# Attention scores contracted over 32 rows in four row groups, with odd score units copied by ScalarE and subtracted by GpSimd

## The reference, cut to what matters

```
for layer in (0, 1):
    h = layernorm(x); Q, K, V = h Wq, ctx Wk, ctx Wv      # 16 heads of width 8
    scores = Q K^T / sqrt(8)    (+ bias[64, 64] and a key padding mask, layer 1 only)
    x = x + tanh(g) * (softmax(scores) V) Wo
    x = x + tanh(g') * ffn(layernorm(x))
```

## Time and profile before

| | us |
|---|---|
| median of 3 executions (190.67 to 191.41) | 191.34 |
| the profiled execution's own time | 190.85 |
| its span in the profile | 189.0 |
| PE busy in the span | 171.1 |
| DVE busy | 146.5 |
| ACT busy | 79.8 |
| POOL busy | 78.5 |

### The profile page before, as it was taken

How to read it: one execution, slowest core, us unless ns; L and a number is a source line. 1 busy time by engine, 2 the same in 40 slices (tenths; PEclk the granted TensorE clock), 3 DMA queues, 4 the chain that set the end, 5 groups by cost and what they waited for, 6 DMA issues and landing times.

```text
span 189.0 us, 4325 instructions
## 1 busy us (share of the span) xinstructions
PE 171.1 (91%) x1606; PEld 95.1 (50%) x1606; DVE 146.5 (77%) x364; ACT 79.8 (42%) x178; POOL 78.5 (42%) x88
## 2 busy tenths in 40 slices
PE   7579869999998979889998969989999998998994
PEld 2134326555577436356665933333555555643593
DVE  0589999889989799285666396799989996769942
ACT  3262355665563252255554001335644556245300
POOL 8429994004043764006666603154674454110000
PEclk9966999999999999999999997999999999999999
DMA  6999999930002010454421030000000000000012
GB/s 163 336 419 350 263 259 235 184 124 2 3 0 24 29 57 30 81 123 77 79 51 31 6 111 3 0 2 2 3 0 3 0 3 0 3 0 0 3 39 72
DMA packets 19558, 15.01 MB, mean 79 GB/s; under 512 B 3493, under 2 KB 18087, under 8 KB 19282
## 3 DMA queue, kind: packets, MB, share of 16 engines
q1 hardware_dynamic: 18370, 13.17, 28.2%
q0 software_dynamic: 736, 1.07, 1.8%
q10 hardware_dynamic: 432, 0.50, 1.1%
HBM read 7.82 MB, written 6.85 MB: 78 GB/s over the span
## 4 chain that ended last, share of the span: by engine, by line
PE 56%; DVE 22%; issue 7%; DMA 5%; POOL 5%; ACT 3%; SPq 0%; POOLq 0%; DVEq 0%
PE bank L878 47%; PE bank L955 6%; DMA xr<-x_in 3%; POOL rstd L311 2%; DVE oT L641 2%; DVE Sa L634 2%; POOL Sx L385 2%; PE bank L1194 2%; DVE Vx L607 2%; DVE mx L636 2%; DVE st L567 1%; DMA big<-sorted_rows 1%; DVE mx L624 1%; DMA sorted_rows<-Pe,slot 1%; ACT xnT L421 1%
## 5 line engine op out<-in xcount | busy, mean ns | idle before, releaser
L878 PE MATMUL bank<-Kx,QT 128*64 128x512 f32 x128 | 35.8, 644 | 2.5 <-DVE Sx L627 2.2
L311 POOL TENSOR_TENSOR rstd<-ve,nhalf 128x2 f32<-128x2 f32 x16 | 11.7, 730 | 54.5 <-DVE ve L573 54.4
L462 ACT ACTIVATE Pe<-Sx 128x512 f32<-128x512 f32 x32 | 20.1, 630 | 24.7 <-POOL Sx L385 15.1
L955 PEld LDWEIGHTS bank<-cst,Pe 128*128 128x128 f32 x128 | 13.5, 140 | 24.3 <-ACT Pe L462 13.0
L373 POOL DMA_INDIRECT routed_rows<-big x15 | 14.8, 984 | 19.7 <-DVE big L843 12.7
L466 ACT ACTIVATE big<-bank 128x512 f32<-128x512 f32 x32 | 18.8, 587 | 8.8 <-PE bank L955 8.7
L955 PE MATMUL bank<-cst,Pe 128*128 128x128 f32 x128 | 20.9, 286 | 0.7 <-ACT Pe L462 0.6
L385 POOL TENSOR_TENSOR Sx<-Sa,mx 128x512 f32<-128x512 f32 x16 | 16.8, 1051 | 11.3 <-DVE mx L636 11.3
L641 DVE RECIPROCAL oT<-bank 128x128 f32<-128x128 f32 x16 | 15.2, 952 | 3.5 <-PE bank L878 3.4
L415 ACT ACTIVATE xn<-xr,nmr,rstd 128x128 f32<-128x128 f32 x20 | 9.2, 486 | 19.4 <-DVE nmr L579 19.3
L878 PE MATMUL bank<-zb 128*32 128x512 bf16 x47 | 14.9, 458 | 2.5 <-DVE bo L598 1.4
(11 more groups left out here) (111 smaller groups left out, 305.2 us busy)
## 6 DMA issues: line engine op xcount, KB each, us to landing
sorted_rows<-empty SPq DMA_DIRECT2D x1, 4686.0 KB, 29.5
wgu<-rgu SPq DMA_DIRECT2D x1, 2048.0 KB, 10.3
wdn<-rdn SPq DMA_DIRECT2D x1, 1024.0 KB, 12.3
big<-sorted_rows SPq DMA_DIRECT2D x15, 66.0 KB, 2.2
ctxT<-ctx_in SPq DMA_DIRECT2D x2, 256.0 KB, 4.6
xr<-x_in SPq DMA_DIRECT2D x2, 256.0 KB, 5.2
wf<-ffn SPq DMA_DIRECT2D x1, 512.0 KB, 5.2
Kx<-KT SPq DMA_DIRECT2D x16, 32.0 KB
```

Of the source, the lines that this page charges most:

```text
L311: pool.tensor_tensor(rstd[:, w], ve[:, w], nhalf[:, w], ALU.pow).then_inc(s_pow, 1)
L462: act.activation(Pe[:, u % 3, :], Sx[:, u % 2, :], ACT.Exp).then_inc(s_exp, 1)
L878: return pe.matmul(o, l, r, start=first, stop=last, **k)
L955: ins = pe.transpose(bank[2 + u % 2][:, m * P:(m + 1) * P], Pe[:, u % 3, m * P:(m + 1) * P], ident)
```

## The change

* K is spread into 4 copies (`HG`) in place of 8: copy j keeps in each group of 32 rows the rows of that group's head j. Q lies once, unpadded. `scores` contracts over 32 rows: a unit is now 4 matmuls (2 row groups by 2 batches) of 256 columns in place of 2 of 512. A unit's 512 columns straddle two PSUM banks, one for each row group (`pair`, `heads`). Even units use row groups 0 and 1 and banks 0 and 1, odd units row groups 2 and 3 and banks 2 and 3. Transposes move to banks 4 and 5; values have one bank (6), output projections bank 7.
* Even units go on as before in both layers (`unit_e`). Odd units are copied out of PSUM by ACT (`score_evac`); in layer 1 POOL adds bias and mask to the copy (`add_bias`); DVE takes the maximum of it (`max_o`); POOL subtracts in both layers (`subtract`).
* PE's order is new: both scores of pair n, odd transposes of pair n-1, values of pair n-1, even transposes of pair n, output projection of pair n-2.
* Both projections of V stand before the first scores; V is cleared at the outset, and the memset of QT is gone. Q's pieces 2 and 3 are projected together. Sorted rows `xs` have a buffer of their own, so the token DMA no longer waits. Banks and waits of later stages are renumbered to match.

```diff
+        pair = [ctx.enter_context(nc.psum_tensor(f"pair{i}", [P, 1024], F32)) for i in range(2)]
+        heads = [pair[i][:, 256:768].rearrange("p (h k) -> p h k", h=HH) for i in range(2)]
...
-            pool.memset(QT[:, :, :], 0.0).then_inc(s_zq, 1)
...
-            pool.memset(Vx[:, 0:HH, :, :], 0.0).then_inc(s_zv, 1)
+            for c in range(CH):
+                pool.memset(Vx[:, c * HH:(c + 1) * HH, :, :], 0.0).then_inc(s_zv, 1)
...
+            def add_bias(n):
+                pool.wait_ge(s_ev, PAIRS + n + 1)
+                sa = Sa[:, n % 2, :].rearrange("p (h k) -> p h k", h=HH)
+                pool.tensor_tensor(sa, sa, mid_bcast(bm[:, n, :], HH), ALU.add).then_inc(s_addo, 1)
+
+            def subtract(layer, n, hh):
+                N = PAIRS * layer + n
+                pool.wait_ge((s_mxe, s_mxo)[hh], (n, N)[hh] + 1)
+                if N:
+                    pool.wait_ge(s_exp, 2 * N - 1 + hh)
+                pool.tensor_tensor(Sx[:, hh, :].rearrange("p (h k) -> p h k", h=HH),
+                                   Sa[:, (2, n % 2)[hh], :].rearrange("p (h k) -> p h k", h=HH),
+                                   last_bcast(mx[:, 2 * hh + n % 2, :], S), ALU.subtract)\
+                    .then_inc((s_sube, s_subo)[hh], 1)
...
+            mask_keys(0, range(HG))
+            mask_keys(1, range(1))
+            rstd_of(0, 2)
+            for n in range(PAIRS):
+                if n == 7:
+                    layer_norm(1)
+                subtract(0, n, 1)
+                if n == 0:
+                    rstd_of(0, 3)
+                    mask_keys(1, range(1, 2))
+                if n == 1:
+                    mask_keys(1, range(2, HG))
+                if n in (2, 3):
+                    residual_base(0, n - 2)
+                if n == 5:
+                    layer_norm(0)
...
+            for n in range(PAIRS):
+                add_bias(n)
+                if n in (5, 7):
+                    rstd_of(3, (n - 5) // 2)
+                subtract(1, n, 0)
+                subtract(1, n, 1)
+                if n in (1, 2):
+                    residual_base(1, n - 1)
...
             def attention(layer):          # ScalarE
+                for n in range(PAIRS):
+                    score_evac(layer, n)
+                    if n >= 1:
+                        pt_evac(layer, n - 1, 1)
+                    exp(layer, n, 0)
...
+                    if n == 6 and layer == 1:
+                        normalise(q, 0)
+                    pt_evac(layer, n, 0)
+                    if n == 7:
+                        xnT_evac(q, 0)
+                        if layer == 0:
+                            xnT_evac(q, 1)
+                        else:
+                            normalise(q, 1)
+                    exp(layer, n, 1)
+                pt_evac(layer, PAIRS - 1, 1)
...
             def attention(layer, step):    # VectorE
+                for n in range(PAIRS):
+                    unit_e(layer, n)
+                    if n in (4, 6):
+                        add_out(layer, n // 2 - 2)
...
+                    max_o(layer, n)
...
+                    if n >= 1:
+                        norm(layer, n - 1)
+                    if n in (4, 6):
+                        out_stats(layer, n // 2 - 2)
...
             def attention(layer, step):    # TensorE
+                for n in range(PAIRS):
...
+                    scores(layer, n, 0)
+                    if n == 0 and layer == 0:
+                        pe.wait_ge(s_kt, CH)
+                    scores(layer, n, 1)
+                    if n == 2:
+                        xn_transpose(2 * layer, 2)
+                        xn_transpose(2 * layer, 3)
+                    if n >= 1:
+                        transposes(layer, n - 1, 1)
+                        values(layer, n - 1)
+                    transposes(layer, n, 0)
+                    if n == 2:
+                        q_proj(layer, 2, 2)
+                    if n == 3:
+                        out_proj(layer, 0)
+                    if n >= 3:
+                        out_proj(layer, n - 2)
...
-            for a in (0, 1):
-                xn_transpose(0, a)
-                q_proj(0, a)
+            xn_transpose(0, 0)
+            q_proj(0, 0)
+            xn_transpose(0, 1)
+            v_proj(0, 0)
+            q_proj(0, 1)
+            v_proj(0, 1)
```

More of the change, by code:

```diff
@@ new lines, in relu1, with score_evac, exp @@
+                act.activation(r1[:, s % 2, :], bank[UP_BANKS[s % 3][1]][:, :], ACT.Relu).then_inc(s_r1, 1)
+            def score_evac(layer, n):
+                act.wait_ge(s_So, PAIRS * layer + n + 1)
+                if n >= 2:
+                    act.wait_ge(s_subo, PAIRS * layer + n - 1)
+                act.activation(Sa[:, n % 2, :].rearrange("p (h k) -> p h k", h=HH), heads[1], ACT.Copy).then_inc(s_ev, 1)
+            def exp(layer, n, hh):
+                u, U = 2 * n + hh, UNITS * layer + 2 * n + hh
+                act.wait_ge((s_sube, s_subo)[hh], PAIRS * layer + n + 1)
+                if U >= 3:
+                    act.wait_ge(s_T, U - 2)
+                act.activation(Pe[:, u % 3, :], Sx[:, hh, :], ACT.Exp).then_inc(s_exp, 1)
@@ L763, in attention @@
                 else:
-                    norm(1, 6)
-                    residual(1, 2)
                     norm(1, 7)
@@ L768, in attention @@
                     step(0)
[L769 removed]
+                    add_out(1, 3)
+                    out_stats(1, 3)
                     mean_rstd(q, 3)
@@ L947, in transposes, with q_proj, scores @@
-            def transposes(layer, u):
-                U = UNITS * layer + u
+            def q_proj(layer, a, n=1):
+                pe.wait_ge(s_xnT, PIECES * 2 * layer + a + n)
+                if layer == 0 and a == 1:
+                    out_bias(0)
+                mm(bank[Q_BANK[layer][a]][:, 0:n * TPP * P], wat[layer][:, WQ:WQ + D],
+                   xnT[:, a * TPP * P:(a + n) * TPP * P]).then_inc(s_qp, n)
+            def scores(layer, n, hh):
+                if n >= 1:
+                    if hh == 1:
+                        pe.wait_ge(s_ev, PAIRS * layer + n)
+                    elif layer == 0:
+                        pe.wait_ge(s_sube, n)
+                    else:
+                        pe.wait_ge(s_adde, n)
+                for g in range(2):
+                    w = slice(32 * (2 * hh + g), 32 * (2 * hh + g + 1))
+                    for r in range(2):
+                        b = 2 * n + r
+                        o = pair[hh][S * r:S * r + S, 256 * (g + 1):256 * (g + 2)]
+                        ins = mm(o.rearrange("p (h k) -> p h k", h=HG), QT[w, b * S:(b + 1) * S],
+                                 Kx[w, :, b * S:(b + 1) * S])
+                ins.then_inc((s_Se, s_So)[hh], 1)
@@ L1043, in attention @@
+                xn_transpose(q, 0)
                 if layer == 0:
-                    out_proj(0, 5)
+                    xn_transpose(q, 1)
                     logits(0)
-                    values(0, 6)
+                    transposes(0, 7, 1)
+                    out_proj(0, 6)
                     ranks(0)
@@ L1066, in attention @@
                 else:
+                    pe.wait_ge(s_xnT, PIECES * q + 1)
+                    keep_warm(XT_BANK[q][0], 3)
+                    transposes(1, 7, 1)
+                    out_proj(1, 6)
+                    values(1, 7)
                     xn_transpose(q, 1)
-                    values(1, 7)
-                    out_proj(1, 6)
                     step(0)
```

379 lines of the change are left out of this document (157 added, 222 removed).

## The result

| | before | changed |
|---|---|---|
| median, 4 executions each (us) | 191.38 | 200.30 (200.17 to 201.16) |
| ratio, 95% interval | | 1.0494 (1.0456 to 1.0531) |
| the profiled execution's time / its span (us) | 190.85 / 189.0 | 200.35 / 198.5 |
| mean granted clock | 0.973 | 0.914 |

The account below looks back on a forecast made before the run. The prediction took PE to bound both attentions before, and layer 1 afterwards to wait on a loop through POOL. 190.85 - 3.3 (layer 0) + 10.2 (layer 1) = 197.75, 198.2 at the median, called 198 us; range 194 to 204.

Parts of the forecast that it names:

- the forecast side: Whole kernel: the change makes it slower; chance 0.89 in all.
- The loop of layer 1: Layer 1: odd scores, copy, add, subtraction, exp, transposes, projection and next scores form one loop, 5.6 us a pair against 4.63.
- the scores of a pair: PE: with row groups overlapping, both units' scores take 0.8 us a pair against 2.02; bounds 0.6 and 1.3.
- The extras: Layer 1, beyond seven steps of 5.6: two `rstd` 1.5, Q's joint projection 1.0, output projections -0.4; all together 41.3 us.
- The price of the add: Layer 1, POOL's `add_bias`: taken at 1.28 us like the residual base; other bound 1.05.
- The clock: Rival, layer 1: PE's waits drop the clock to half, some 6 us more over half the layer, around 204; chance 0.17.
- The forecast case: Layer 1: loop on POOL at 5.3 to 5.9 us a step, full clock, total 195 to 201; chance 0.66.
- Layer 0: First scores to last values 41.5 us instead of 47.3 (-5.8), first scores 2.5 later for V and bias projections; net -3.3.
- The ends of layer 1: First scores to transposes 4.6 against 4.95; Q's single evacuation -0.5; last even transposes to feed-forward 6.6 against 5.37.
- The range: Total, 8 in 10: 194 to 204; layer 1 ends +8.2 (add 1.05, pair 0.6) and +12.5 (pair 1.3).
- Serial row groups: Rival, PE: row groups don't overlap, scores stay at 2.0 us a pair, +1.2 for each of 16 pairs, 217; chance 0.04.
- A cheap POOL: Rival, layer 1: POOL's add and subtraction cost 0.69 us each, loop 4.65, total 190.5; chance 0.13 including a misjudged path.

Follow-up runs that it names:

- w1: Changed kernel plus fillers (short matmuls on cleared data that keep TensorE busy) ahead of TensorE's two waits in each step of layer 1; 1.0270 of the kernel before.
- ow: Changed kernel with o1's order in layer 1 plus fillers ahead of TensorE's waits there, fewer than in w1; 1.0200 of the kernel before.
- o1: Changed kernel, layer 1 reordered only: next pair's scores and odd copy go ahead of this pair's even transposes and their copy; 1.0094 of the kernel before.
- b2: Changed kernel's operations with layer 1 laid out over one more step as a longer pipeline, no fillers; 0.9813 of the kernel before (187.37 us).
- a0: The changed kernel run again, unaltered, as the measure for the other runs; 1.0482 of the kernel before.
- w0: Changed kernel plus fillers at the start of layer 0 only, ahead of pair 0's transposes and the values of pairs 0 and 1; 1.0362 of the kernel before.
- p1: Changed kernel with POOL's order in layer 1 turned round: even subtraction ahead of the odd unit's add of mask and bias; 1.0320 of the kernel before.
- pw: p1 with the fillers of w1 in layer 1; 1.0443 of the kernel before.

## Why the prediction was right, and where its terms were off

Forecast 198.0, measured 200.3, within the range of 194 to 204 and on the forecast side. By its own steps:

**The loop of layer 1: right, and shown.** The step was forecast at 5.6. With the clock held up (w1) a plain one is 5.35, and seven with their extras 39.75 against the 41.3 of the prediction. Of the 0.25, 0.20 is one link: the sum has transposes, output projection and scores, 0.59 + 0.41 + 0.8 + 0.1 = 1.9, from even transposes to the copy of the odd scores, and ACT's own list sets 1.70 there. The price in that link, the scores of a pair, was too high by itself: 0.8 in the sum, 0.62 in ow, from the start of the scores to the next matmul (144.69 to 145.31; the record of 0.69 overlaps it). By the rule of the Trainium skill that the prediction cites (TensorE: Matmul & The Clock Gate, "Measured speedup vs the span model") the estimate was 0.6, and this trace agrees with it, with 0.62 for 16 records of 256 columns in four row groups.

The extras came out at 2.26 where the prediction has 2.1: two `rstd` 0.68 each, Q's projection 0.74 (forecast 1.0), and 0.16 for two output projections at n = 3. The prediction's -0.4 for these should be -0.8 by its own count (5 projections in seven steps, not 7), and neither showed, because the projection isn't on the path at full clock: steps with one and without one are 5.35 and 5.36. The price of the add, the other open one, was taken at 1.28 and is 1.27. That the loop runs through the order of the lists, not through the operations as such, is shown by o1 and b2, which keep every operation and are 3.9% and 6.7% below a0.

**The clock: a rival that came true in part.** The forecast case had layer 1 at full clock and gave the falling clock 0.17, with some 6 us. It fell, to a mean of 0.81 over the seven steps (0.74 in a0), and costs some 4 us: 4.1 in the seven steps (43.83 against 39.75 in w1), 4.0 by the ratios of w1 and a0 (2.1%, with intervals of 0.5 to 0.8 either way). That is the main reason for the 2.3 above the forecast: +4.1 for the clock, less 1.6 for the seven steps at full clock (39.75 in place of 41.3). That the total is so near is in part luck, since these two errors go against each other. The step that failed is "full clock" in the forecast case, not the loop. The prediction had the rows for it: a microsecond with PE at 0.08 and one with nothing ahead of the falls at 10 and 113, and it forecast waits of 1.3 in each pair.

**Layer 0: the net right, its two terms both off.** Forecast -3.3, measured -3.6. The first scores came 0.6 later, not 2.5. The projections of V fell into gaps of PE and ran at full clock, one in 1.15, and ended at 13.70. But from there to the last values it took 43.1, not 41.5, and the prediction's own parts of the 41.5 add up to 40.8 only (2.9 + 5.6 + 4.7 + 4.8 + 4.6 + 3 x 4.3 + 5.3). The first two steps are 7.1 and 5.8 where it has 5.6 and 4.7. In part that is the clock, at half between about 17.5 and 27, with waits of 2.17 and 2.00 ahead of the transposes of pair 0; w0, at full clock, has the first four steps 1.3 shorter. The rest is ACT's list: with a normalisation (17.61) and a copy of V (18.12) ahead of it, ACT copied the even transposes of 16.56 only at 18.80, and the odd exp came at 19.29; w0 has the same times within 0.04 and a first step of 6.9, fillers included. The late steps, 4.23 and 4.33, are the 4.3 of the prediction.

**The ends of layer 1.** First scores to first transposes 4.47 (forecast 4.6, before 4.95); last even transposes to the feed-forward 6.75 (forecast 6.6, before 5.37). The 0.5 for one evacuation of Q in place of two did not come: the first scores of layer 1 are 3.8 ahead of before, hardly more than the 3.6 at the end of layer 0's values. Together 12.3 - 0.5 + 1.4 = 13.2 for layer 1, against the forecast 10.2.

**The range.** Its two ends for layer 1 are not what their conditions give. An add of 1.05 and a pair of 0.6 shorten each of seven steps by 0.43, which makes 7.2 of the 10.2 and not 8.2; a pair of 1.3 lengthens each by 0.5, 13.7 and not 12.5. The range would have been about 193 to 204.5.

**The other rivals.** Serial row groups: no, 0.69 for a pair. A cheap POOL: no, 1.27 and 1.05. Of the experiments' own theories, the one that POOL's order alone is at fault fell with p1 and pw.

## What to carry to other kernels

An operation that is cheap by the busy columns can be dear by its place. Here a copy of 0.6 and an add of 1.27 went to two engines with time to spare, under a new order of TensorE's list, and seven steps became 8 us longer, 12 with the clock: in each pair they stood, ahead of the even subtraction, between scores and even transposes, and the next scores stood behind these on TensorE's list, as the next copy did on ScalarE's. When work is moved to idle engines, close the loop by hand through every list it passes, and shift the lists by a step until each wait has other work under it. Look for the second path too: here ScalarE's list came to the copy 0.17 later than the path that the sum went by, and POOL's turned order only moved the loop to VectorE's list. The shift turned +4.9% into -1.9% with the same operations. Fillers helped where TensorE waited (w1, 2.1%), and cost their own length where it had no idle time (ow, 0.6 a step).

## What the runs showed of the hardware beyond that

Between 136 and 158 in the changed kernel the granted clock fell and came back once in each step. Each fall came directly behind a microsecond with next to nothing on TensorE: 0.00 busy from 139 to 140 and from 146 to 147, 0.05 from 153 to 154. The longest wait of this stretch is 1.63, and TensorE's records cover 15.3 of its 22 us. But such a wait doesn't always bring the clock down. In w0, whose layer 1 has the same lists, TensorE waits 1.43 ahead of 142.16, with nothing at all from 141 to 142, and 1.66 ahead of 153.81, and the clock stays at 1.00; only behind the next wait of 1.66, at 165.31, is it at half. What decides between the two, no run here shows.

In w0 TensorE stopped for 1.34 us in the middle of 32 value matmuls that wait for nothing, and in w1 for 0.68 in the same group of its list, after 23 of them. The profile calls it "issue". Its cause was not tried.
